# Two-layer graph attention on one core: which units take the adjacency itself as operand, and a fourth PSUM bank for the first chunk's transposes

## The reference, cut to what matters

```python
# layer 0, for each head h
Wh = (x @ W).reshape(N, H, D)                       # N 4096, H 4, D 32
e = s_src[:, None, :] + s_dst[None, :, :]           # s = Wh . a
e = jnp.where(e >= 0, e, 0.2 * e)                   # leaky relu
e = jnp.where(adj[:, :, None] > 0, e, NEG_INF)
attention = softmax(e, axis=1)
x = layernorm(x + elu(attention @ Wh))
# layer 1: x_tan = logmap0(x); the same attention with one head on x_tan;
# x = layernorm(x + proj(expmap0(attention @ x_tan)))
```

## Time and profile before

| | |
|---|---|
| median of three runs | 905.64 us |
| the profiled execution | 904.97 us |
| its span, first to last instruction | 903.2 us |
| mean granted TensorE clock, share of full speed | 0.982 |
| busy: PE, DVE, ACT | 839.6, 769.3, 682.5 us |
| chain that ended last | PE 52%, DVE 28%, ACT 13%, issue 6% |
| L694 matmuls (layer 0) | 8192, in two forms: 99 columns and 198 columns |
| L668, the XOR | 76 of 128 units, 1225 ns each |

### The profile page before, as it was taken

The page is one execution under the profiler, slowest core; times in us unless marked ns, Lnnn a source line. Parts: engine busy times, 40 slices in busy tenths (PEclk is TensorE's granted clock), DMA queues, the critical chain, the costliest instruction groups (busy, mean ns, idle before and its releaser), DMA issues.

```text
span 903.2 us, 24394 instructions
## 1 busy us (share of the span) xinstructions
PE 839.6 (93%) x10868; PEld 684.7 (76%) x10868; DVE 769.3 (85%) x1318; ACT 682.5 (76%) x803; POOL 43.4 (5%) x80
## 2 busy tenths in 40 slices
PE   8588999989999889999998998799999999999995
PEld 6588999988999889999998984455555555555552
DVE  3978889899988999889999999785878687878876
ACT  3999998899999999999995875778364554728222
POOL 3200000000000000000000000000000000000000
PEclk9799999999999999999999999899999999999998
DMA  8999377804657226214031011430335353544000
GB/s 147 178 106 236 70 76 90 235 26 39 82 72 171 114 25 80 40 44 170 26 119 25 2 36 60 71 105 13 117 94 168 113 188 121 181 142 139 1 12 14
DMA packets 42065, 84.67 MB, mean 94 GB/s; under 512 B 6242, under 2 KB 31332, under 8 KB 41316
## 3 DMA queue, kind: packets, MB, share of 16 engines
q0 software_dynamic: 12416, 33.56, 26.5%
q1 hardware_dynamic: 29540, 49.50, 15.3%
HBM read 112.27 MB, written 21.12 MB: 148 GB/s over the span
## 4 chain that ended last, share of the span: by engine, by line
PE 52%; DVE 28%; ACT 13%; issue 6%; DMA 0%; SPq 0%; DVEq 0%; ACTq 0%
PE bank L694 25%; PE bank L1305 21%; ACT masks L773 7%; DVE ring L658 4%; DVE ring L638 4%; ACT ring L625 3%; PE bank L1295 2%; DVE ring L668 2%; DVE ring L662 2%; PE bank L541 2%; DVE evac L710 2%; ACT masks L528 2%; ACT moving L578 1%; DVE second_part L493 1%; PE bank L1234 1%
## 5 line engine op out<-in xcount | busy, mean ns | idle before, releaser
L694 PE MATMUL bank<-moving,ring 128*128 128x99 bf16 (+1 forms) x6528 | 451.0, 218 | 14.5 <-DVE ring L668 10.7
L694 PEld LDWEIGHTS bank<-moving,ring 128*128 128x128 fp8e4 x6528 | 386.8, 97 | 17.5 <-DVE ring L668 12.3
L625 ACT ACTIVATE ring<-s_rows,scores 128x1024 fp8e4<-128x1024 f32 x360 | 380.4, 1142 | 0.7 <-ACT ring L625 0.7
L694 PE MATMUL bank<-moving,masks 128*128 128x99 bf16 x1664 | 221.5, 208 | 8.2 <-DVE ring L658 4.1
L1305 PE MATMUL bank<-moving,masks 128*128 128x387 bf16 x1056 | 178.2, 327 | 0.0
L694 PEld LDWEIGHTS bank<-moving,masks 128*128 128x128 fp8e4 x1664 | 162.4, 98 | 10.7 <-issue 5.8
L773 ACT ACTIVATE masks<-s_rows,adj_tiles 128x512 fp8e4<-128x512 f32 x256 | 157.9, 710 | 0.6 <-DVE moving L751 0.5
L1305 PEld LDWEIGHTS bank<-moving,masks 128*128 128x128 fp8e4 x1056 | 101.7, 96 | 73.0
L658 DVE SCALAR_TENSOR_TENSOR ring<-ring,masks 128x1024 int32<-128x1024 int32 x90 | 109.6, 1218 | 8.1 <-ACT ring L625 8.0
L668 DVE TENSOR_TENSOR ring<-masks,ring 128x1024 int32<-128x1024 int32 x76 | 93.1, 1225 | 25.2 <-PE bank L694 23.4
L400 ACT ACTIVATE ring<-ring 128x4 f32<-128x4 f32 (+1 forms) x24 | 4.9, 205 | 136.4 <-DVE ring L316 110.7
(11 more groups left out here) (214 smaller groups left out, 633.0 us busy)
## 6 DMA issues: line engine op xcount, KB each, us to landing
masks_kept<-masks SPq DMA_DIRECT2D x4, 4096.0 KB, 17.5
masks<-masks_kept SPq DMA_DIRECT2D x8, 2048.0 KB, 9.8
adj_tiles<-in_adj_dram POOLq DMA_DIRECT2D x24, 512.0 KB, 8.4
s_rows<-score_rows SPq DMA_DIRECT2D x14, 512.0 KB, 5.8
ring<-masks_kept POOLq DMA_DIRECT2D x11, 512.0 KB, 3.9
first_part<-masks_kept POOLq DMA_DIRECT2D x11, 512.0 KB, 3.9
second_part<-masks_kept POOLq DMA_DIRECT2D x10, 512.0 KB, 3.8
adj_tiles<-in_adj_dram POOLq DMA_DIRECT2D x16, 256.0 KB, 13.2
```

Source lines behind the costliest of these rows:

```text
L625: last = act.activation(j_tile(below, k), s_rows[:, h % 2, :], ACT.Sign, bias=scores[:, g * JU + k, h:h + 1], saturate=False)
L694: last = pe.matmul(acc_bank(c, h, b)[:, at + lo:at + hi], mask, moving[:, j, h, lo:hi], start=first, stop=(j == T - 1), skip_group_check=True)
```

## The change

Four edits.

1. The list `DIRECT`. Chunk 0: heads 2 and 3 have two and one direct units where each had three (units 0.2.3, 0.3.1 and 0.3.3 are no longer direct). Chunks 1 and 2: heads 0 to 3 have 5, 3, 1, 1 direct units where each head had 2 (new: units 3, 4, 6 of head 0 and unit 3 of head 1; gone: unit 1 of heads 2 and 3). Chunk 3 is as before. Over all 53 of 128 units are direct where 52 were.
2. `QUARTER_BANKS` = 4: the transposes of chunk 0's quarters take banks 4 to 7 in turn and not 5 to 7, and `turn_quarter` waits for the copy four turns back and not three.
3. `turn_group` waits for at least all 16 quarter copies before its first group.
4. `pe_unit` waits in unit 0.1.0 for all 16 quarter copies, since bank 4 is taken for sums there.

```diff
-    ACC_BANKS, TURN_BANKS = 5, 3
+    ACC_BANKS, TURN_BANKS, QUARTER_BANKS = 5, 3, 4
...
-              "DDDDDDDD" "DD-D----" "DD-D----" "DD-D----"
-              "DD------" "DD------" "DD------" "DD------"
-              "DD------" "DD------" "DD------" "DD------"
+              "DDDDDDDD" "DD-D----" "DD------" "D-------"
+              "DD-DD-D-" "DD-D----" "D-------" "D-------"
+              "DD-DD-D-" "DD-D----" "D-------" "D-------"
               "DD-DD-D-" "DD-DD-D-" "DD-DD-D-" "DD-D-D--"]
...
         def turn_bank(n):
-            return bank[ACC_BANKS + n % TURN_BANKS]
+            return bank[8 - QUARTER_BANKS + n % QUARTER_BANKS] if n < Q else bank[8 - TURN_BANKS + n % TURN_BANKS]
...
-                if n >= TURN_BANKS:
-                    pe.wait_ge(turned_out, n - TURN_BANKS + 1)
+                if n >= QUARTER_BANKS:
+                    pe.wait_ge(turned_out, n - QUARTER_BANKS + 1)
...
-            pe.wait_ge(turned_out, c * Q + q - TURN_BANKS + 1)
+            pe.wait_ge(turned_out, max(Q, c * Q + q - TURN_BANKS + 1))
...
+                if c == 0 and h == 1 and g == 0 and t == 0:
+                    pe.wait_ge(turned_out, Q)
```

## The result

The changed kernel takes 898.96 us (median of 6; 897.82 to 900.68) against 905.49 us (6 runs; 904.97 to 906.58) for the kernel before. The ratio is 0.9925, 95% interval 0.9915 to 0.9936: 6.5 us faster by the medians and 6.8 by the ratio, where 8.4 was forecast and 894.0 to 901.3 us stated as the range. The profiled execution took 899.25 us with a span of 897.3.

A forecast was written before the change was run, and what follows sets the result against it. TensorE was taken as busiest overall, VectorE as bound in heads 1.0 and 2.0. TensorE's terms summed to 10.7 us, but ScalarE's limit of 8.5 gave 8.4: 904.97 - 8.4 = 896.6 profiled, 897.2 in runs; range 894.0 to 901.3.

The forecast's parts named there:

- ScalarE's part: End of chunk 2: ScalarE's unchanged work lets unit 3.0.0 be ready at most 1.9 + 4.0 + 2.6 = 8.5 us earlier.
- TensorE's own sum: Up to unit 3.0.0: TensorE gains 2.3 + 1.5 + 2.1 + 2.7 + 2.1 = 10.7 us, less 1 us there.
- The price of a direct unit: All chunks: a direct unit costs TensorE 1.24 us more and saves VectorE one XOR, about 1.25 us with hand-over.
- Heads 0 and 1: Chunks 1 and 2: four more direct units each cost 5.0 us against TensorE waits of 6.7 and 7.7; gain 1.5 and 2.7.
- Heads 2 and 3: Chunks 1 and 2: one direct unit fewer per head saves TensorE 2.5 us per chunk, 2.1 after new waits of 0.2 per head.
- Rival B: Lightened heads 2 and 3: VectorE takes back a microsecond each, chunk 0 gives nothing; gain 3 to 4 us; 0.18 with rival E.
- Chunk 0: Heads 2 and 3: three direct units fewer save TensorE 3.7 us, of which 2.3 was taken, bounds 0 to 3.7.
- the fourth bank: Chunk 0, head 0: removes TensorE's waits for quarter copies, covered by ScalarE's unchanged order; taken as 0, -1 to +1 us.
- Rival A: End of chunk 2: ScalarE doesn't bind, TensorE alone sets it; gain 9.7 to 11 us, time 895.3; chance 0.12.
- Chunk 3 and layer 1: After chunk 2: as before, the chain crosses the boundary on VectorE, so all 8.4 us should pass to the end.
- rival E: Head 0.0: TensorE idles more, lower clock comes for three stretches, not one; 3.4 us lost, time 900.6; 0.18 with Rival B.
- Rival D: Heads 0 of chunks 1 and 2: TensorE runs out of instructions, about 5 us a place, up to 912 us; chance 0.05.

The follow-up runs named there:

- ScalarE relieved: Sign unit 2.1.5 moved from ScalarE to VectorE, against the changed kernel's list with three banks: 896.08 us, ratio 0.9892 to the kernel before.

## Why the prediction was right

The time fell into the range, and ScalarE's part was foreseen at the right place. The number came near for a reason that holds only in part: TensorE's own sum was too large, and with what it really gained TensorE and ScalarE reach the end of chunk 2 together. Gains by TensorE's unit starts, in the two profiles:

| stretch | taken in the prediction | kernel before to changed kernel |
|---|---|---|
| up to unit 0.1.0 (the bank) | 0 | -1.2 |
| head 0.1 (no stretch at the lower clock) | 0 | +0.7 |
| heads 0.2 and 0.3 | 2.3 | 1.4 |
| chunk 1 | 3.6 | 3.2 |
| chunk 2 | 4.8 | 4.3 |
| TensorE's start of unit 3.0.0 | 10.7 | 8.3 |
| unit 3.0.0 ready, by ScalarE's limit | 8.4 | 7.4 |
| chunk 3 | 0 | -1.3 |
| layer 1 | 0 | -1.1 |
| span | 8.4 | 5.9 |

**The price of a direct unit** held. Head 1.0 came out at 30.52 us where 26.6 + 3.7 = 30.3 had been worked out. The estimate from the Trainium skill's page TensorE: Matmul & The Clock Gate, section Back-to-back issue gap, is contradicted: by it head 1.0 would have fallen to about 27.5. (The step between the page's two spacings is 50 ns over 384 columns, so my estimate should have been 13 ns for 99 columns and not 8, 0.4 us for a direct unit and about 27.8 us for head 1.0; the trace excludes that as well.)

**Heads 0 and 1** of chunks 1 and 2: the waits for L668 in head 0 are gone, as said. They gave 1.4 and 2.5 us for 1.5 and 2.7. (6.7 of waits less 5.0 is 1.7, so the 1.5 of the prediction was a slip.)

**Heads 2 and 3:** the small new waits for an XOR at unit 3 are there. TensorE of the changed kernel, units 0.3.2, 0.3.5 and 1.2.3:

```profile
154.52 3.05 PE L696 MATMUL bank<-moving,ring 128*128 128x99 bf16 x64 [0.58 <-DVE ring L668]
164.35 0.85 PE L696 MATMUL bank<-moving,ring 128*128 128x99 bf16 x15 [0.57 <-DVE ring L668]
...
247.17 0.99 PE L696 MATMUL bank<-moving,ring 128*128 128x99 bf16 x18 [0.22 <-DVE ring L668]
```

They are the waits at 0.3.2 and 0.3.5 (0.5 to 0.8 expected), and 0.2 in each of heads 1.2 and 2.2. Heads 2 and 3 gave 1.8 per chunk for 2.1. Rival B, VectorE taking back a microsecond in each head, is excluded by them.

**Chunk 0** gave less than the 2.3 taken. Heads 0.2 and 0.3 together took 60.4 to 60.8 us in the four profiled executions with the old list of chunk 0, and 59.4 (median; 58.5 to 61.0) in the ten with the new one, so about 1.3. The prediction left out a stop of TensorE in unit 0.3.7, for nothing that the profile shows, which grew. Before and after:

```profile
173.98 1.84 PE L694 MATMUL bank<-moving,ring 128*128 128x99 bf16 x37 [0.84 <-issue]
173.16 1.84 PE L696 MATMUL bank<-moving,ring 128*128 128x99 bf16 x37 [1.64 <-issue]
```

It was 0.5 to 0.9 us long in the four executions with the old list and 0.8 to 2.2 (median 1.64) in the ten with the new one. What it is stays open. In the changed kernel's profile TensorE starts unit 1.0.0 only 0.8 earlier, because the late quarter costs 1.2 more.

**ScalarE** was late where the prediction said, and by about as much: VectorE waited 1.2 us for signs in units 2.3.7 and 3.0.0 (1 to 3 expected). Its three terms in the profile of the changed kernel: 1.3 of the `elu_exp` (178.87 to 177.58) for 1.9, 3.6 between it and the signs of 3.0.0 (403.96 to 399.07, less the 1.3) for 4.0, 2.5 of slack for 2.6. The sum is 7.4 for 8.4 or 8.5. The first term is short because of **the fourth bank, taken as 0**: its cover was to be ScalarE's unbroken order, and this cover had a gap, since the order includes copies of a quarter that comes by DMA. I reasoned that nothing lands earlier and did not ask whether something could land later. The copies of that quarter came 1.2 to 1.3 us later in this execution. Part of it was given back ahead of chunk 1, as the lower clock of 84.90 did not come. With three banks, counted from the first quarter copy, the first term is 1.8 and unit 3.0.0 is ready 8.5 us earlier than before, as worked out.

What the prediction had wrong is what this limit is worth. It held TensorE's 10.7, less 1, against ScalarE's 8.4, and took the whole difference as lost. TensorE reached 8.3 in this execution (9.3 with three banks, counted from the first quarter copy), and its wait at unit 3.0.0 is 0.32 us for the 0.30 of before. With ScalarE relieved chunks 1 and 2 are not shorter at all; heads 3.0 and 3.1 are, by 0.65. So Rival A, ScalarE not binding, is half right: TensorE sets the end of chunk 2 as much as ScalarE does. Its number, a gain of 9.7 to 11, failed because it used the same sum for TensorE.

**Chunk 3 and layer 1** did not pass the gain on whole. Counted from TensorE's start of unit 3.0.0, 1.3 us went in chunk 3: 0.7 in heads 3.0 and 3.1, where VectorE has lost its 0.9 us in hand, and 0.6 in head 3.2 with its stop. In layer 1 it was 1.1 us, with the lower clock at 576.3. That is rival E's mechanism at another place, with one stretch. A stretch of 3.4 us came there in four of the twelve executions of the experiments that have a profile, two of them with the old list in chunks 1 and 2, and not in the other eight, so it belongs to the spread. Over all fourteen profiles the time from the last matmul of layer 0 to the end was 366.5 to 366.7 us in the five with the stretch and 365.5 to 365.8 in the nine without. A forecast by one profile can't be better than that: 6.5 and 9.2 us of gain were measured for the same changed kernel in two sets of runs. That the second of them is nearer to the 8.4 is no merit of the sum.

**Rival D** did not come in chunks 1 and 2: TensorE's stop in unit 3.2.2 is there again, a little longer, and the one in unit 0.3.7 above is a second place, without a stretch at the lower clock behind it.

```profile
479.75 0.25 PE L696 MATMUL bank<-moving,ring 128*128 128x99 bf16 x2 [3.09 <-issue]
```

No such stop over 0.3 us appeared in chunk 1 or 2 in any of the fourteen profiles, although TensorE ran heads 1.0 and 2.0 without a pause. Whether TensorE was short of instructions at either stop, as rival D has it, no run tested.

## What to carry to other kernels

Work that can be moved between two engines belongs where the other one waits: the number of direct units hardly changed (52 to 53), and 6 to 9 us came from where they stand. When two engines are evened out this way, add up the third one's order over the same stretch first, since its spare time (here 6.6 us over two chunks) limits what it can follow. Then compare that limit with what the first engine can really reach: here the two came out equal, the third engine stood on the chain with 21%, and taking 4.2 us off it was worth only 0.65 us. A share of the chain is not the time that can be won there. A buffer that lets an engine finish earlier also moves every request that hangs on it; here the bank moved one by 3 us, and whether that made the transfer ahead of it later stays open.

## What the runs showed of the hardware that I had not expected

The second quarter, 1 MB asked for at 9.3 us, was in use at 36.0 to 38.2 us in the nine executions in which a 2 MB write was asked for at 26.0 to 26.7, at 33.8 to 34.1 in the three in which it was asked for at 27.0 to 27.5, and at 33.7 and 34.0 in the two in which it was held back until the quarter had landed. So a write asked for less than a microsecond later hardly mattered. After one and the same wait of TensorE at the start of layer 1 (1.94 us, ending at 575.97 in the changed kernel) the clock went to its lower level for 3.4 us in five of fourteen executions, the changed kernel's first two among them, and stayed up in the other nine. The wait was 1.94 to 3.15 us long in the five and 1.57 to 2.43 us in the nine, so its length alone doesn't decide. The 64 matmuls behind it took 12.43 us and not 10.77. TensorE stopped for nothing that the profile shows at the same two places in all fourteen executions, 0.5 to 2.2 us in unit 0.3.7 and 1.5 to 3.8 us in unit 3.2.2, and only behind the second did the clock go to its lower level, for 3.4 us in nine executions and 6.8 in five.
